# Storing intermediate tensors in the order in which they are produced, in a one-core block of triangle, recurrence and scan layers

## The reference, cut to what matters

```python
x = x + L0_conv(ln(x))    # triangle: bimc,bmjc->bijc
x = x + L0_ffn(ln(x))     # experts over pooled tokens
x = x + L1_conv(ln(x))    # triangle with a mask
x = x + L1_ffn(ln(x))     # recurrence over 512 time steps
x = x + L2_conv(ln(x))    # scan over 128 rows, 9-tap convolution
x = x + L2_ffn(ln(x))     # recurrence
x = x + L3_conv(ln(x))    # triangle: bikd,bjkd->bijd
x = x + L3_ffn(ln(x))     # router and 8 experts

def triangle(z):          # L0, L1, L3
    zn = layernorm(z)
    a = sigmoid(zn @ Wga + bga) * (zn @ Wla + bla)      # L1: times a mask
    b = sigmoid(zn @ Wgb + bgb) * (zn @ Wlb + blb)
    k = einsum(a, b)                                    # one 128x128 product per channel
    return sigmoid(zn @ Wgo + bgo) * (layernorm(k) @ Wlo + blo)

def recurrence(x):        # R1, R2: batch norm over x @ W.T, then
    y[t] = sigmoid(wx[t] + y[t-1] @ V.T)

def scan(x):              # rows of the image, one after the other
    new = row + relu(conv1d(carry, W))
```

## Time and profile before

| | us |
|---|---|
| three runs, median (lowest, highest) | 577.54 (576.71, 581.73) |
| profiled execution, from the first to the last instruction (its only time given) | 576.0 |
| PE busy in it | 446.6 |
| DVE busy | 364.1 |
| POOL busy | 244.8 |
| ACT busy | 238.6 |

### The profile page before, as it was taken

One profiled execution on the slowest core, in us unless ns is written; L12 is line 12 of the kernel. 1 busy time (PEld: TensorE's weight loads), 2 busy tenths in 40 slices (PEclk: granted clock), 3 DMA queues, 4 the chain that ended last, 5 costly groups with the idle time before them and its releaser, 6 DMA issues.

```text
span 576.0 us, 8603 instructions
## 1 busy us (share of the span) xinstructions
PE 446.6 (78%) x3020; PEld 344.4 (60%) x3020; DVE 364.1 (63%) x1214; ACT 238.6 (41%) x573; POOL 244.8 (43%) x309
## 2 busy tenths in 40 slices
PE   3698867977698856897479986799579857909996
PEld 2356643775346633896369974499445846805664
DVE  5798584717796486005934468600979399398885
ACT  1496545211575554672530004567369542200000
POOL 2697395001585295000320003200259388119995
PEclk9999989768798999798759997999779986558999
DMA  9300000000000000000000000000000000001223
GB/s 170 64 2 1 1 1 1 0 2 0 2 1 1 1 2 0 2 1 1 1 0 1 2 1 1 1 2 1 1 1 2 1 1 1 0 0 19 38 38 55
DMA packets 34106, 6.03 MB, mean 10 GB/s; under 512 B 33644, under 2 KB 33772, under 8 KB 34029
## 3 DMA queue, kind: packets, MB, share of 16 engines
q1 hardware_dynamic: 34062, 5.46, 5.5%
HBM read 3.36 MB, written 2.10 MB: 9 GB/s over the span
## 4 chain that ended last, share of the span: by engine, by line
PE 49%; DVE 32%; POOL 10%; ACT 5%; issue 2%; DMA 1%; SPq 1%; DVEq 0%; POOLq 0%
PE psum L1275 7%; DVE ab L669 6%; PE psum L1037 5%; DVE moments L292 5%; PE psum L1036 5%; DVE ab L657 4%; PE psum L400 4%; POOL x_cols L734 3%; POOL z L338 3%; POOL gate L729 3%; PE psum L1448 3%; PE psum L554 3%; DVE z L302 2%; PE psum L1426 2%; PE psum L1057 2%
## 5 line engine op out<-in xcount | busy, mean ns | idle before, releaser
L400 PE MATMUL psum<-ident,z 128*128 128x128 f32 x256 | 55.3, 359 | 42.9 <-POOL z L338 40.3
L400 PEld LDWEIGHTS psum<-ident,z 128*128 128x128 f32 x256 | 39.0, 185 | 70.8 <-POOL z L338 57.9
L524 PE MATMUL psum<-wp_L,z_t 64*128 64x320 f32 x384 | 65.5, 470 | 3.4 <-ACT z_t L323 2.1
L338 POOL TENSOR_TENSOR z<-z,stats 128x496 f32<-128x496 f32 (+1 forms) x40 | 41.5, 1037 | 60.3 <-DVE z L302 60.3
L292 DVE BATCH_NORM_STATS2 moments<-x_cols 128x6 f32<-128x64 f32 x448 | 61.9, 213 | 4.6 <-POOL x_cols L734 4.3
L335 POOL MEMSET z<- 128x16 f32 x32 | 4.0, 126 | 123.4 <-DVE z L302 123.4
L323 ACT ACTIVATE z_t<-psum 128x512 f32<-128x512 f32 x56 | 40.1, 722 | 37.5 <-PE psum L400 37.2
L524 PEld LDWEIGHTS psum<-wp_L,z_t 64*128 64x128 f32 x384 | 33.1, 191 | 31.0 <-issue 27.6
L338 POOL TENSOR_TENSOR z<-x_cols,stats 128x512 f32<-128x512 f32 x24 | 25.1, 1050 | 61.3 <-DVE stats L298 61.1
L1128 ACT ACTIVATE ab<-psum,mv 128x128 f32<-128x128 f32 x112 | 41.2, 368 | 18.3 <-PE psum L1037 7.5
L1037 PE MATMUL psum<-ab,R_vt 128*128 128x128 f32 x224 | 47.9, 297 | 0.0
(11 more groups left out here) (249 smaller groups left out, 942.5 us busy)
## 6 DMA issues: line engine op xcount, KB each, us to landing
x_cols<-in_x_dram SPq DMA_DIRECT2D x16, 128.0 KB, 3.0
out_dram<-x_cols SPq DMA_DIRECT2D x32, 64.0 KB, 1.9
par<-in_par_dram SPq DMA_DIRECT2D x1, 644.5 KB
w<-in_w_dram SPq DMA_DIRECT2D x1, 264.0 KB
w<-in_w_dram SPq DMA_DIRECT2D x1, 256.0 KB
mask<-in_mask_dram SPq DMA_DIRECT2D x1, 64.0 KB
row<-in_row_dram SPq DMA_DIRECT2D x1, 3.3 KB
w2l<-in_w2l_dram SPq DMA_DIRECT2D x1, 2.0 KB
```

Of the source, the lines that this page charges most:

```text
L338: pool.tensor_tensor(Z4[:, r, :, 0:c], values[:, r, :, 0:c], RSTD[:, q].unsqueeze(3).to_broadcast([N, SQ, G, c]), ALU.mult).then_inc(L.s[" ...
L400: m = pe.transpose(bank(b % 2)[:, k * N:(k + 1) * N], block_of(Z)(4 * b + k), ident[:, :])
L524: m = pe.matmul(bank(slot_bank(s) + h, 2 * 5 * C), ZT[rows, s, :], wp[l][rows, :, :], start=True, stop=True)
```

## The change

Four tensors get the layout in which their producer writes contiguously, and the readers take the stride. AB becomes (n, w). The copies after the product write to PROD (the memory of SQR) as (g, c, s), and the turn that follows reads every 32nd element; the squares move from SQR to the upper half of AB, whose contents are no longer needed. ZT keeps its block order in r1 and r2 too, so that the recurrence's columns of one time step are now 128 elements apart in s. RIN becomes (n, i), and the row steps read with a step of 128 elements. All instructions, waits and their order on each engine stay; only addresses and the tiles named change.

```diff
+        PROD = SQR
+        SQUARES = AB[:, NC:2 * NC]
...
-        ABt = AB[:, :].rearrange("p (a c n) -> p a c n", a=2, c=C)
+        ABt = AB[:, :].rearrange("p (n a c) -> p a c n", a=2, c=C)
...
-                if L is r1 or L is r2:
-                    dst = ZTIME[:, :, 4 * q:4 * q + 4].rearrange("p n s -> p s n")
...
+        def product_of(t):
+            rows = t[:, :].rearrange("p (f s) -> p s f", s=S)
+            return lambda s: rows[:, s, :]
...
-                    m = pe.transpose(bank(b % 2)[:, k * N:(k + 1) * N], block_of(Z)(4 * b + k), ident[:, :])
+                    m = pe.transpose(bank(b % 2)[:, k * N:(k + 1) * N], product_of(PROD)(4 * b + k), ident[:, :])
...
-            out = Z[:, :].rearrange("p (s g c) -> p c g s", g=G, c=C)[:, 4 * b:4 * b + 4]
-            src = bank(KB[b % 4]).rearrange("p (c g s) -> p c g s", c=4, g=G)
+            out = PROD[:, :].rearrange("p (g c s) -> p g c s", g=G, c=C)[:, :, 4 * b:4 * b + 4, :]
+            src = bank(KB[b % 4]).rearrange("p (c g s) -> p g c s", c=4, g=G)
...
-            return AB[:, :].rearrange("p (w g s) -> p g s w", g=G, s=S)[:, :, s, :]
+            return AB[:, :].rearrange("p (g s w) -> p g s w", g=G, s=S)[:, :, s, :]
...
-        ZTIME = ZT[:, :, :].rearrange("p s f -> p (s f)").rearrange("p (n s) -> p n s", s=S)
+        ZTIME = ZT[:, :, :].rearrange("p s n -> p n s")
...
-                pe.matmul(bank(AS_FREED[b % 6]), W["wraw"][:, :], ZTIME[:, :, 4 * b:4 * b + 4], start=True, stop=True)\
+                pe.matmul(bank(AS_FREED[b % 6]), W["wraw"][:, :], ZT[:, 4 * b:4 * b + 4, :], start=True, stop=True)\
...
-        RIN = GATE[:, :].rearrange("p (i n) -> p i n", i=N)
+        RIN = GATE[:, :].rearrange("p (n i) -> p i n", i=N)
```

More of the change, by code:

```diff
@@ L613, in out_square @@
                 act.wait_ge(L.s["o_ps"], L.at["o_ps"] + b + 1)
-                act.activation(SQR[:, b * BANK:(b + 1) * BANK].rearrange("p (s h f) -> p h s f", s=4, h=2),
+                act.activation(SQUARES[:, b * BANK:(b + 1) * BANK].rearrange("p (s h f) -> p h s f", s=4, h=2),
                                o_bank(b)[:, :, :, 1, :], ACT.Square).then_inc(L.s["o_sq"], 1)
@@ L688, in out_sum @@
                 dve.tensor_reduce(stats[:, 2, 16 * b:16 * b + 16],
-                                  SQR[:, b * BANK:(b + 1) * BANK].rearrange("p (n c) -> p n c", c=C), AX.X, ALU.add)\
+                                  SQUARES[:, b * BANK:(b + 1) * BANK].rearrange("p (n c) -> p n c", c=C), AX.X, ALU.add)\
                     .then_inc(L.s["o_sum"], 1)
```

## The result

The changed kernel takes 614.4 us (median of 4 runs, 612.94 to 616.69), the kernel before 578.33 (4 runs, 576.71 to 581.73): the ratio is 1.0606 [1.0568, 1.0645]. 568.0 was forecast, in a range of 563 to 575. The profiled execution spans 613.7 us against 576.0, 37.7 more. Most lines have moved by four: L1036 is now L1040, L554 is L558, L657 is L661, L669 is L673, L591 and L593 are L595 and L597, L1326 is L1330; L323 keeps its number.

The account below looks back on a forecast made before the run. No single engine was taken to bound the kernel; the bound walks from stage to stage. Gains of 5.6 + 0.75 + 1.05 + 2.3 less 0.2 made 9.5 us: 576.0 - 9.5 + 1.5 = 568.0 us, range 563 to 575.

Parts of the forecast that it names:

- The readers on PE decide the sign: TensorE's stepped reads in recurrence and triangle product (L1036, L554): between 0 and 48 us more, taken as 0.
- the 115 of the bound: Upper bound per TensorE record with stepped moving columns: 128 x 0.9 = 115 ns, on 416 records of L1036 and L554.
- first rival: L1036 and L554: PE pays for stepped columns as ACT and DVE for writes; 48 us, total 616 us; chance 0.12.
- 9.5 us of gains: Whole kernel: 5.6 + 0.75 + 1.05 + 2.3 - 0.2 us less time.
- t1's main loop: DVE's 128 products in t1 (L657): 193 ns from start to start falls to 150, 5.6 us less.
- not set by its write: Rival on t1's product: DVE time is saved only at the edges, 3.9 us in all, 573.6 us; chance 0.08.
- the scan's longer read: Scan's row step on DVE (L1326): 0.09 us more, 56 times, 5.3 us of DVE time, hidden by idle time, so 0.
- The copies of L323: ACT's copies of the turned layer norm in r1, sc, r2: 1.06 to 0.60 us, five in the chain, 2.3 us less.
- The copies after the product: Copies of PSUM banks behind each triangle's product: only the last bank shows, three times 0.35 us, 1.05 us less.
- the turn behind them: Turn after the copies, loading every 32nd element as weights: 0 to 16 ns more per record, taken as 0.
- t3's loop: Main loops of t0 and t3: DVE's product (L669) 0.19 us shorter, loops keep their length; 0.75 us less for both.

## Why the prediction was wrong

**The step that failed first: "The readers on PE decide the sign ... I take 0."** The bounds there were 0 and 48 us, and the 0 rested on the weights as the nearest row. Weights turned out to be the exception: at 16 bytes and more the moving operand pays 106 to 121 ns per 128 columns, the weights 2 to 38. The loads in L1044 told nothing of the other operand, though both pass through the same engine. The measured cost is 18.7 us in L558 and 18.5 in L1040, 37.2 us, thus 89 ns on each of the 416 records. It is below the 115 of the bound since a record paid 95 ns (r1: 0.42 less 0.23 us for two) to 106 (t3: 6.8 us over 64) at full clock and nothing at the lower. The forecast's first rival, priced at 616 us, had the place and the mechanism; I gave it 0.12. That its time came within 2 us of the measured one is partly luck: its 48 us were 11 too many, while the 9.5 us of gains set against them came to 3.7, with 3.9 us of further losses (scan 1.9, L372 0.9, t0's loop 1.1). The rows that bore on a stepped operand, ACT's writes, DVE's writes and DVE's reads the earlier trace rows, all showed a price; the rows without it came from an operand of another kind. That should have put this rival near the forecast. Even the weights were not quite free: at 256 bytes, a step for which the earlier trace rows has no row, L372 lost 0.9 us where the sum had nothing.

**The second: t1's main loop, 5.6 us.** L661 shortened by 46 ns, against 43 forecast, and its spacing did not move. The text named the right doubt ("an operand for the mask comes from memory") and then argued that the 193 ns left no more than half for what is fixed. That argument added times for reading and writing within one element, while the mask's column as an operand set the spacing: 192 ns with it and 131 with a constant, whatever the step. A shorter duration is no shorter spacing. The rival "not set by its write" had 0.08.

**The third: the scan's longer read, 0.** L1330 takes 372 ns (385 forecast), 80 more. The scan became 1.9 us longer, all of it in steps like these, DVE's timeline in the scan after (its idle time ahead in brackets):

```profile
347.59 0.37 DVE L1330 SCALAR_TENSOR_TENSOR ab<-psum,gate 128x128 f32<-128x128 f32 x1 [0.35 <-PE psum L1279]
...
348.99 0.37 DVE L1330 SCALAR_TENSOR_TENSOR ab<-psum,gate 128x128 f32<-128x128 f32 x1 [0.35 <-PE psum L1279]
```

Two steps, one of each stream, take 1.40 us where they took 1.34. So 50 of the 80 ns were hidden and 30 were not. DVE's idle time was not all slack: a stream's next products wait for its own DVE step, and with a longer step that wait shows. In the second piece of the scan TensorE's records start 112 ns apart in both kernels, save behind the 31 that wait for a DVE step: there the next start comes after 143 ns in the mean, 114 before. 31 x 29 ns is 0.9 us, which is what this piece lost (22.69 against 21.75).

**What held.** The copies of L323: in r1, sc and r2 the stages ahead of the steps became 0.73, 0.54 and 1.50 us shorter, 2.8 together (2.3 forecast, from five copies; the earlier trace rows shows four, and the fifth stands in the same chain at 366.46 us), no copy is over 598 ns now, the eight of the scan among them (1064 before). The copies after the product reached 692 and 597 ns, but their 1.05 us came to about 0.6, since the turn behind them lost 0.06 for every four records, a price that the prediction quoted from the earlier trace rows and then left at 0. L673 fell to 425 ns and t3's loop kept its length but for 0.3 us at the edges. These 3.7 us are inside the 614.4.

## What to carry to other kernels

A stride does not vanish when it moves from the writer to the reader: count how often each end passes over the data and which end lies on the path. Here each factor is written once, beside other work, and read once as the moving operand in a stretch where TensorE had no idle time. Where both ends matter, store two float32 neighbours of either order together: at 8 bytes neither paid more than a little (636 ns against 597 for the copy, 288 against 287 for the product), though in the kernel's time the gain was too small to be told. And read the spacing of a row of instructions, not the duration of one, before pricing what a shorter instruction gives.

## What the runs showed of the hardware

- TensorE's moving operand in float32, 128 columns at full clock: 112 ns at steps of 4 bytes and 114 at 8, 173 at 12, 218 to 233 from 16 bytes on, up to 256 bytes. In the kernel a stepped record took about 0.21 us at either level of the clock, and a plain one 0.21 at 1.2 GHz and 0.115 at 2.4, so at 1.2 GHz the step cost nothing.
- TensorE's weights, 128 rows of a turn: 2.09 us for 16 at a step of 16 bytes against 1.93 contiguous, 2.14 at 252 bytes, 2.51 at 256.
- A product on VectorE with a scalar from a column in memory: 192 ns apart for 64 elements, 131 with a constant, at either step of the write.
